# A convolution, attention and feed-forward kernel on one core: attention stage written out and reordered

## What is computed

```python
x = x + conv11x11_depthwise(groupnorm(x))        # kernels built from 4 cones
h = layernorm(x) @ w_attn                        # q, k, v; q and k get RoPE
wei = softmax(causal(q @ k.T * 16 ** -0.5))      # 16 images x 6 heads, 256 x 256
x = x + (wei @ v) @ w_proj
y = gelu(bitlinear(layernorm(x), W1, b1))        # signs of centred weights, clipped at
y = bitlinear(y, W2, b2)                         # the absolute maximum of a group of images
out = x + y                                      # NCHW
```

## Time and profile before

| | value |
|---|---|
| median of the runs | 301.82 us |
| the profiled execution | 304.61 us, span 302.9 us |
| granted TensorE clock, mean | 0.943 of full speed |
| PE, DVE, ACT, POOL busy | 81%, 70%, 45%, 38% of the span |
| stage A with its set-up | 0 to about 105 us |
| attention up to its step 1 | to 131.8 us |
| its steps 1 to 13 | 131.8 to 215.2 us |
| its steps 14 to 17 and the first group's products | to 243.2 us |
| rest of the feed-forward stage | to 302.9 us |

### The profile page before, as it was taken

How to read it: one execution, slowest core, us unless ns; L and a number is a source line. 1 busy time by engine, 2 the same in 40 slices (tenths; PEclk the granted TensorE clock), 3 DMA queues, 4 the chain that set the end, 5 groups by cost and what they waited for, 6 DMA issues and landing times.

```text
span 302.9 us, 6111 instructions
## 1 busy us (share of the span) xinstructions
PE 244.4 (81%) x1880; PEld 184.5 (61%) x1880; DVE 211.0 (70%) x645; ACT 137.3 (45%) x318; POOL 115.0 (38%) x121
## 2 busy tenths in 40 slices
PE   0129898999999877589988799889988589999880
PEld 0118898988898755357666567777644344555440
DVE  0898548687778599947776556777625667988943
ACT  1321246455545433437665556656663134245330
POOL 1460524675566636243332222333288413110110
PEclk9999999999999989559999989999997969999997
DMA  4910100000089900124443435343000000101102
GB/s 128 252 27 1 28 26 26 4 26 26 3 135 116 90 0 4 31 47 83 93 96 90 95 83 101 79 92 65 1 2 1 0 2 0 39 0 39 42 23 68
DMA packets 25449, 15.61 MB, mean 52 GB/s; under 512 B 3473, under 2 KB 25298, under 8 KB 25426
## 3 DMA queue, kind: packets, MB, share of 16 engines
q1 hardware_dynamic: 23568, 14.04, 24.1%
q10 hardware_dynamic: 1858, 1.29, 1.9%
HBM read 4.26 MB, written 1.57 MB: 19 GB/s over the span
## 4 chain that ended last, share of the span: by engine, by line
PE 54%; DVE 14%; SPq 13%; issue 8%; DMA 4%; ACT 3%; POOL 2%; DVEq 0%; ACTq 0%; POOLq 0%
PE bank L1245 10%; SPq L372 10%; PE bank L1498 8%; PE bank L1512 7%; PE bank L1271 5%; PE bank L1386 3%; DVE qr_ring L907 3%; SPq L388 3%; PE bank L1344 3%; PE bank L1260 3%; PE bank L1361 2%; DMA stack<-nmax_t 2%; DMA rad_bc<-in_L_conv_radius 2%; DVE rest_ring L881 2%; PE bank L1347 2%
## 5 line engine op out<-in xcount | busy, mean ns | idle before, releaser
L956 DVE TENSOR_REDUCE nmax<-bank 128x1 f32<-128x128 f32 x192 | 55.0, 349 | 29.0 <-PE bank L1347 28.8
L488 POOL TENSOR_SCALAR_AFFINE_SELECT pt_ring<-pt_ring 128x512 f32<-128x512 f32 x48 | 31.1, 648 | 68.2 <-ACT pt_ring L665 68.1
L665 ACT ACTIVATE pt_ring<-bank 128x384 f32<-128x384 f32 x96 | 41.8, 487 | 23.1 <-PE bank L1363 22.3
L1245 PE MATMUL bank<-xs_ring,toep 128*128 128x192 f32 x256 | 49.9, 340 | 0.6 <-issue 0.6
L1245 PEld LDWEIGHTS bank<-xs_ring,toep 128*128 128x128 f32 x256 | 44.2, 199 | 2.2 <-issue 0.9
L1344 PE MATMUL bank<-stack 96*128 96x128 bf16 x192 | 34.6, 257 | 3.9 <-DVE nmax L956 3.5
L1347 PE MATMUL bank<-mask,ident 128*128 128x128 bf16 x192 | 34.5, 227 | 0.0
L459 POOL TENSOR_TENSOR parts<-rest_ring,parts 96x512 bf16<-96x512 f32 x16 | 25.0, 1562 | 21.5 <-DVE parts L884 21.5
L1361 PE MATMUL bank<-stack 97*128 97x256 bf16 x96 | 23.4, 287 | 11.8 <-DMA stack<-nmax_t 7.8
L1498 PE MATMUL bank<-parts,w_b 97*128 97x512 f32 (+1 forms) x60 | 26.5, 573 | 3.4 <-DVE parts L1112 2.2
L1512 PE MATMUL bank<-parts,w_b 128*96 128x512 f32 (+1 forms) x60 | 23.3, 493 | 0.9 <-issue 0.9
(11 more groups left out here) (154 smaller groups left out, 483.8 us busy)
## 6 DMA issues: line engine op xcount, KB each, us to landing
stack<-parts SPq DMA_DIRECT2D x96, 96.0 KB, 3.4
x_ring<-in_x SPq DMA_DIRECT2D x8, 192.0 KB, 2.4
out<-xs_ring SPq DMA_DIRECT2D x5, 288.0 KB, 2.6
stack<-in_x SPq DMA_DIRECT2D x2, 384.0 KB, 6.4
stack<-in_x ACTq DMA_DIRECT2D x2, 384.0 KB, 11.2
stack<-nmax_t SPq DMA_DIRECT2D x32, 1.5 KB
cst<-in_const SPq DMA_DIRECT2D x1, 384.0 KB, 11.7
w_in<-in_L_ffn_W ACTq DMA_DIRECT2D x2, 144.0 KB
```

Of the source, the lines that this page charges most:

```text
L488: nc.gpsimd.affine_select(out=v, in_=v, compare_op=ALU.is_ge, fill=0.0, base=0, pattern=[[0, 2], [0, 2], [1, P]], channel_multiplier=-1).t ...
L665: nc.scalar.activation(pt_ring[:, s, h, :], bank[:, 3 + h % 2, 0:T + P], ACT.Exp, scale=float(HD) ** -0.5).then_inc(s_exp, 1)
L956: last = nc.vector.tensor_reduce(nmax[:, n0 % 2, HEADS * t + h:HEADS * t + h + 1], bank[:, h % 3, first:first + (t + 1) * P], op=ALU.max, ...
L1245: nc.tensor.matmul(dst, w, xs_ring[:, s, p, k].rearrange("p b c -> p (b c)"), start=(k == 0 and p == 0), stop=False)
```

## The change

The attention steps are written out (no hardware loop) and reordered on all streams:

- scores_q and maxima work on image n + 3 in step n, in two groups of three heads. One reduction takes the maxima of three heads at once, so an image has four reductions. The products of a group wait until the group before has been reduced.
- The two row transfers of an image are issued by POOL, for image n + 2 in step n. SP issues only the 96 image transfers, and image b waits for the scores_k of image b - 6.
- transpose_max works on image n + 2 and writes into bank 5; transpose_norm writes into spare columns of banks 3 and 4, between the products of scores_k.
- The last convolution pair is interleaved with the scores of image 0; the work of the last pair's q, k and v is spread over attention steps 0 to 4.
- The sums of the weights, their centring and signs, and three memsets move into stage A's steps 2 to 5.
- `second_stats(0)`, `second_rstd(0)`, `second_norm(0)` and `second_norm(1)` move into steps 9, 10 and 12; the first group's transposes and products go in between steps 13 and 15 and just behind; the attention ends interleaved with them.

```diff
-                wait(sp, s_sk, HEADS * (b - RING + 2))
-            def max_row(i, n0):
-                b, slot = n0 + RING * i, n0 % RING
-                wait(sp, s_mtc, b + 1)
-                for t in range(NT):
-                    sp.dma_start(stack[KROWS:KROWS + 1, slot, :, 0, t * P:(t + 1) * P],
-                                 nmax_t[t * HEADS:(t + 1) * HEADS, n0 % 2, :]).then_inc(s_mrow[slot], 16)
+                wait(sp, s_sk, HEADS * (b - RING + 1))
...
+            for b in range(B):
+                stack_image(b)
...
+            def max_row(b):
+                slot = b % RING
+                pool.wait_ge(s_mtc, b + 1)
+                for t in range(NT):
+                    nc.gpsimd.dma_start(stack[KROWS:KROWS + 1, slot, :, 0, t * P:(t + 1) * P],
+                                        nmax_t[t * HEADS:(t + 1) * HEADS, b % 2, :]).then_inc(s_mrow[slot], 16)
+            def step_b(n):                               # POOL
+                select(n, 0)
+                if n + 2 < B:
+                    max_row(n + 2)
+                select(n, 1)
...
+                if n == 9:
+                    second_rstd(0)
+                if n == 10:
+                    second_norm(0)
+                if n == 12:
+                    second_norm(1)
+                select(n, 2)
...
-                last = nc.vector.tensor_reduce(nmax[:, n0 % 2, HEADS * t + h:HEADS * t + h + 1],
-                                                   bank[:, h % 3, first:first + (t + 1) * P],
-                                                   op=ALU.max, axis=AX.X, negate=True)
+                    first, k = t * P, HEADS * t + 3 * g
+                    last = nc.vector.tensor_reduce(nmax[:, b % 2, k:k + 3], bank[:, 0:3, first:first + (t + 1) * P],
+                                                   op=ALU.max, axis=AX.X, negate=True)
...
+            def step_b(n):                               # DVE
+                if n >= 2:
+                    normalise_o(n - 2)
+                if n in (3, 4):
+                    second_parts(0, PAIRS - 1, n - 3)
+                if n + 3 < B:
+                    maxima(n + 3, 0)
...
+                if n >= 3:
+                    add_attention(n - 3)
+                if n + 3 < B:
+                    maxima(n + 3, 1)
...
+                if n == 9:
+                    second_stats(0)
...
+                wait(pe, s_max, 2 * b + g)                 # scores_q(b, g)
+                if b >= 4:                                 # transpose_max(b)
+                    pe.wait_ge(s_on, b - 3)
...
+            def step_b(n):                               # PE
+                scores_k(n, 0)
+                if n + 3 < B:
+                    scores_q(n + 3, 0)
+                if n + 2 < B:
+                    transpose_max(n + 2)
+                scores_k(n, 1)
+                weighted_values(n - 1)
+                if n + 3 < B:
+                    scores_q(n + 3, 1)
+                if n in (2, 3):
+                    pe.wait_ge(s_o, n)
+                    transpose_qk(0, PAIRS - 1, n - 2)
+                scores_k(n, 2)
+                if n >= 2:
+                    project_out(n - 2)
+                transpose_o(n - 1)
...
+            transpose_x2(0, 0)                             # PE, behind step 13
+            transpose_x2(0, 1)
+            step_b(B - 2)
+            first_product(0, 0, 0)
+            first_product(0, 0, 1)
+            step_b(B - 1)
+            first_product(0, 0, 2)
+            for k in range(HC):
+                first_product(0, 1, k)
...
+            transpose_norm(B - 2, t)
+            weighted_values(B - 1)
```

More of the change, by code:

```diff
@@ L1060, in bounds @@
+            maxima(1, 1)
+            second_parts(0, n - 1, 0)
+            rotate(0, n - 1, 1)
+            maxima(2, 0)
+            maxima(2, 1)
+            for n in range(B - 1):
+                step_b(n)
             def bounds(rows, shared, gmax, lim, signal, count):
@@ L1464, in _ @@
[L1464 to L1476 removed]
+            pe.wait_ge(s_tok, n)
@@ new lines, in _ @@
+            project_qkv(0, n, 0)
+            transpose_max(1)
+            scores_q(2, 0)
+            transpose_qk(0, n - 1, 1)
+            scores_q(2, 1)
+            pe.wait_ge(s_tok, PAIRS)
+            pe.wait_ge(s_lt, PAIRS)
+            scores_k(0, 0)
+            scores_q(3, 0)
+            project_qkv(0, n, 1)
+            scores_k(0, 1)
+            scores_q(3, 1)
+            transpose_max(2)
+            scores_k(0, 2)
+            for n in range(1, B - 2):
+                step_b(n)
```

564 lines of the change are left out of this document (267 added, 297 removed).

## The result

The changed kernel takes **293.28 us**, the median of four executions (291.8 to 296.59), where the kernel before takes 301.67 beside it: a ratio of 0.9668, 95% interval 0.961 to 0.9725. Measured a second time, six executions beside eleven of the kernel before, it is 293.91 us and 0.9682 (0.9635 to 0.973). The ratios leave out executions in a slower state that any kernel falls into now and then (the one of 296.59 us here, three of the four in experiment 2), so they are not the quotients of the medians. The forecast was 290.0, with a range of 285.0 to 297.5.

What follows compares the result with a forecast made beforehand. DVE was taken to bound the start and SP's transfer queue most attention steps. Terms -7.1 - 1.9 - 2.7 = -11.7 us, from the median of 301.8, gave 290.1, said as 290; range 285 to 297.5.

Steps and rivals of the forecast that it cites:

- The last step of the sum: Whole kernel: from 292.9 us on the profiled execution to 290, using the median of 301.8 us minus 11.7.
- Stretch 1: From 93.3 us to attention step 1: DVE paces it, less DVE work makes it 7.1 us shorter.
- The weights' centring and the memsets ... lie in DVE's idle time: Stage A: this moved work is covered there, taking 2.8 to 3.1 us off DVE before step 1.
- a rival that keeps the whole stretch at 38.5: Start up to attention step 1: not shortened, with max_row(0) on POOL ahead of sines; 297 us, chance 0.10.
- Stretch 2: Attention steps 1 to 13: terms 25.0 + 52.7 + 3.0 + 0.8 = 81.5 against 83.4 us, minus 1.9.
- The mechanism for a plain step: Plain attention steps: scores_q on PE alternate with maxima on DVE, 4.15 + 1.42 + 0.3, 5.85 us taken.
- The stall of POOL: Steps 9 and 10: the last select waits behind second_rstd(0), 2.4 us plus 0.6 from second_norm(0), 3.0 us.
- The 0.8 us for the moved transposes: Steps 1 to 13: six first-group transposes moved ahead of step 14 add 0.8 us.
- PE's own 5.8 us: Attention steps: PE's own content of a step, read from the chain, stays 5.8 us since no product is dropped.
- The two rivals with POOL as the bound: Attention steps: row issues on POOL pace them; 301 us at 2.27 a row, 310 at 2.6; chance 0.07 each.
- The rule that I weighed: Rows on POOL: VectorE can lock out descriptor writing; 3.1 us a row would give 8.2 us a step, slower.
- Stretch 3: Step 14 to the second group's first product: first products fill gaps, 28.0 to 25.3 us, minus 2.7.

Runs made afterwards that it cites:

- experiment 2: Changed kernel with its rows issued by SP again, row b-3 ahead of image b: three executions of 294.8 to 297.0 us, one of 289.68.
- experiment 5: Changed kernel with weight centring, memsets and sign activations moved from the convolution stage into attention steps 5 to 8: 292.25 us, ratio 0.9654.
- experiment 6: Changed kernel, three rows on SP, second_stats(2) behind clips: 294.0 us; with one-head reductions and later power: also both edits 288.77, only row 0 on SP 286.72, ACT rows 287.28.
- experiment 7: Changed kernel with one-head reductions and later power, plus 40 unused PE products where PE waits for DVE: 288.86 us, ratio 0.9545.
- experiment 8: Changed kernel repeated unaltered beside the kernel before: 293.91 us; its profiled execution 293.76 us.
- experiment 3: Changed kernel with one reduction per head and 128-block instead of one over three heads: 288.80 us, ratio 0.9533.
- experiment 4: Changed kernel with second layer norm's power and first normalisation one step later: 290.22 us, ratio 0.9606; with reductions over one head too: 287.44 us, 0.952.
- experiment 1: Kernel before with only its rows issued by POOL, SP keeping the images: 295.83 us, ratio 0.9764.

## Why the prediction was right or wrong

**The total (290.0 against 293.3).** On the profiled execution the forecast was 292.9 and 291.8 came. The last step of the sum took the 2.8 us by which before's profiled execution lay over its median off the forecast too, which supposed that the changed kernel's profile would lie as far over its median. It lay 1.5 us under it, and in the repeat at it. That is the miss in the time: a difference of two traces carries the luck of both. And that the traces themselves differ by nearly the forecast is luck as well: the start gave too little, and the clock of the kernel before gave about 5 us to stretches 2 and 3 that no term of the sum foresaw.

**Stretch 1, -7.1 forecast, -2.7 measured.** The sum had 24.1 us of DVE busy and 7.2 idle; measured are 27.3 and 8.5. Three terms failed.
- "The weights' centring and the memsets ... lie in DVE's idle time": they had cover on DVE, but cost 2.4 us all the same (experiment 5). With them three rotations came just behind POOL's third parts instead of just ahead of them, and took 0.9 us longer each. Of the 2.4 us the table shows 1.5, because this execution was 0.95 us ahead of the one before at the fourth rotation. I had named the full 3 us as the price without cover, and not looked at who shares with DVE.
- The rows on POOL ahead of the sines of image 13. I carried this only as a rival that keeps the whole stretch at 38.5. It cost 1.1 us on DVE's side, through the rotation beside it (experiments 2 and 6).
- The granted clock: 0.73 from 110 to 122.55 us. I forecast nothing for it, and named it among what would make the prediction wrong. With rows on SP and full clock, the stretch from the last convolution to step 1 is 30.6 us (126.32 less 95.72) against 30.1 in my sum (124.7 less the 94.62 of the kernel before). In the changed kernel it is 33.0; less the 1.1 us of the issues, 1.3 us are left, which I put down to the fall (argued, for the order of the image transfers differs too). What a fall costs depends on its place: with the fall nearer to step 1, or with a second one, the kernels of experiments 5, 7 and 8 take 1.3, 1.5 and 1.5 us more from the last convolution to step 1.

These three, 1.5, 1.1 and 1.3 us, and 0.5 us that I can't place make up the 4.4 us.

The reductions themselves came as priced, 1.42 a pair.

**Stretch 2, -1.9 forecast, -6.0 measured.** The mechanism for a plain step was the right one, and the hops were over-priced: 4.08 us of PE, 1.43 of DVE and 0.16 for the hand-overs, 5.68, against 4.15 + 1.42 + 0.3. Over steps 5 to 13 that and the two shorter last steps (5.36 and 5.3) are 2.2 us. Steps 1 to 4 came at 24.8 against 25.0. The stall of POOL was in the place that I named, and 2.1 us instead of 3.0, for step 9 ended 0.5 late and step 10 waited 1.5. The 0.8 us for the moved transposes does not show. So each of the four terms of the 81.5 was priced too high, 4.1 us together. That PE's idle time fell by 2.5 us, near the forecast of 1.9, is luck: the 1.9 is 83.4 less 81.5, and the 83.4 hold about 3.5 us of low clock that the 81.5 do not. What was wrong without consequence here is "PE's own 5.8 us": it is at most 5.38 (experiment 3). I had read a chain that stays on PE from 139.48 to 145.43 as PE's content, though an engine can be on the chain and still stretch its work to the pace of what it feeds. That a forecast with it came near is luck, since the alternation was as long.

**The row.** 0.52 us each instead of 1.0, below the nearest rows of POOL and of SP; 26 of them take 13.7 us in steps 1 to 13. Landing takes 3.3 us in the median, against 2.14 from SP. The two rivals with POOL as the bound needed 1.95 us; they are refuted by the price. The rule that I weighed, from the Trainium skill (DMA: Bandwidth & Descriptors, SWDGE vs HWDGE vs iDMA), did not show on the row: the mean of the 26 is 0.53 us. That does not refute it, for I had taken its price from a copy, and DVE ran mostly reductions and sums here. What showed is the other direction. The Trainium skill (SBUF — State Buffer, section SBUF: two separate sides) says that a DVE operation with two SBUF inputs and a GpSimd operation that reads SBUF exclude each other, and that the one which starts second waits; the rotation's 1.75 us beside a third part, the third part's 1.71 us behind a rotation and the statistics of experiment 4 beside a select agree. The 2.89 us say that the issue of a row also keeps DVE out.

**Stretch 3, -2.7 forecast, -4.7 measured.** The kernel before with rows on POOL alone already had 1.7 of it (28.00 to 26.29). The rows are not the reason: from step 14 to the first group's first product both kernels take 15.58 us. The 1.7 us lie in the first six products, 4.51 us at the lower clock against 2.81. The rest, 3.0, is the ends merged, near to the 2.7 of the sum.

**Which part of the change did what.** The issuing engine alone 7.1 us (experiment 1). The two traces lie 8.6 us apart: 3.3 of these are shorter waits in steps 1 to 13, and about 5.2 are the clock, which stood higher; whether the shorter waits kept it there is not shown. Order and merged ends, with reductions over one head kept, another 7 (0.9764 to 0.9533). The reductions over three heads cost 4 us of it back. These shares hold for adding the parts in this order: taken out of the changed kernel, the rows on POOL may be worth nothing, since one execution of experiment 2 took 289.68 us without them. Forecast was the opposite weight: most from the start, little from the steps, and the wide reductions as part of the gain.

## What to carry to other kernels

Where two engines alternate, what counts on the consumer is the work left after the producer's last item, not its sum: a fused operation that must wait for the whole group can lose to six small ones that begin early, though it takes less busy time. Issue a small late transfer from a queue in which nothing urgent stands behind it and nothing long ahead, and ask for it early enough that its latency is no part of the loop. Before work is moved into the idle time of one engine, look at what its neighbours then do beside it; a small shift can put it behind an operation that excludes it, here in two or three steps. And before a difference of two traces is put down to waits, split it into the engine's idle time and its busy time at the granted clock.

## What the runs showed of the hardware

- A row of 1.5 KB issued by POOL occupies it for 0.52 us and lands 3.3 us later (medians); by ACT 0.67 us, by SP 0.73 to 0.77.
- A DVE sum of two SBUF operands (0.83 us) takes 1.75 us if it starts with a two-input operation of POOL, and 2.89 if POOL goes on with two row issues. If the sum starts first, it is POOL's operation that takes 1.71 us instead of 1.15.
- Two operands on DVE are held by POOL even where both are short: 0.17 us became 0.55 beside a select.
- The granted clock fell to its lower level near the start of attention in every kernel profiled here but the one with its rows on SP, where it fell some 60 us later. Small changes moved the fall by up to 9 us (from 113 to 122), and a fall nearer to step 1, or a second one, cost 1.3 to 1.5 us, which is more than several of the edits are worth.
- At the lower level six products of the feed-forward stage took 4.51 us, and 2.81 at full clock.
